# Epsilon folded into the variance aggregate, two-tensor row scalings and new instruction orders in a two-layer language-model tower

## The reference

```python
h = _L0_tok_ref(...)                      # word + position + type rows, layer norm (E), gamma, beta
h = h + _L0_attn_ref(_layernorm(h), ...)  # P: random-feature attention, 16 heads, 44 features
h = h + _L0_ffn_ref(_layernorm(h), ...)   # F: top-2 of 32 low-rank experts
h = h + _L1_attn_ref(_layernorm(h), ...)  # R: rotary causal softmax attention, 16 heads
h = h + _L1_ffn_ref(_layernorm(h), ...)   # M: ternary-weight MLP 256 -> 1024 -> 256
```

## Time and profile before

| | |
|---|---|
| median of 3 runs | 469.33 us (463.96 to 470.93) |
| the profiled execution: span from first to last instruction | 470.3 us (the page gives no other time of it) |
| TensorE busy | 401.4 us (85%) |
| VectorE busy | 366.7 us (78%) |
| GpSimd busy | 284.0 us (60%) |
| ScalarE busy | 257.9 us (55%) |

### The profile page before, as it was taken

The page is one execution under the profiler, slowest core; times in us unless marked ns, Lnnn a source line. Parts: engine busy times, 40 slices in busy tenths (PEclk is TensorE's granted clock), DMA queues, the critical chain, the costliest instruction groups (busy, mean ns, idle before and its releaser), DMA issues.

```text
span 470.3 us, 13968 instructions
## 1 busy us (share of the span) xinstructions
PE 401.4 (85%) x5026; PEld 273.4 (58%) x5026; DVE 366.7 (78%) x969; ACT 257.9 (55%) x573; POOL 284.0 (60%) x399
## 2 busy tenths in 40 slices
PE   8988768868898888799979797989898979797885
PEld 3444344535565667475747475656666656565664
DVE  4478899977999786999979698687878887766552
ACT  1246474547576555577738374647474736373541
POOL 7778888967577667677867655454555335252120
PEclk9998999979999899999989898898989998999999
DMA  4797542346464648455866484583767664611001
GB/s 135 183 291 189 144 102 26 70 100 106 102 118 92 116 91 140 106 119 96 138 113 107 96 121 88 94 152 68 95 104 127 116 91 74 101 36 24 13 13 35
DMA packets 145843, 48.55 MB, mean 103 GB/s; under 512 B 137264, under 2 KB 143216, under 8 KB 145776
## 3 DMA queue, kind: packets, MB, share of 16 engines
q1 hardware_dynamic: 144144, 43.21, 49.2%
q0 software_dynamic: 1632, 4.46, 3.4%
...
...
## 4 chain that ended last, share of the span: by engine, by line
PE 32%; issue 20%; DVE 15%; POOL 14%; DMA 9%; SPq 5%; ACT 4%; another core or an unknown queue 1%; POOLq 0%; DVEq 0%; ACTq 0%
PE PS L1415 11%; PE PS L2004 4%; PE PS L1925 2%; PE PS L2022 2%; DMA qkT<-qs 2%; DMA rTm<-split 2%; POOL split L695 2%; DMA rT<-split 1%; PE PS L1767 1%; PE PS L1626 1%; DVE xnR L1039 1%; DMA emb_type<-in_type,ids 1%; POOL qe L666 1%; SPq L534 1%
## 5 line engine op out<-in xcount | busy, mean ns | idle before, releaser
L1075 DVE TENSOR_REDUCE split<-PS 128x16 f16<-128x2048 f32 x16 | 36.8, 2297 | 10.3 <-PE PS L1494 7.6
L692 POOL TENSOR_TENSOR stage_f<-stage_f 128x512 f32<-128x512 f32 x16 | 21.0, 1310 | 27.7 <-DVE stage_f L1056 10.9
L1155 ACT ACTIVATE xTR<-PS 128x256 f16<-128x256 f32 x16 | 6.1, 382 | 49.6 <-PE PS L1805 49.6
L2004 PE MATMUL PS<-xTM,w1q 128*128 128x128 f16 x512 | 31.4, 219 | 0.0
L2004 PEld LDWEIGHTS PS<-xTM,w1q 128*128 128x128 f16 x512 | 28.6, 98 | 3.6 <-issue 3.6
L685 POOL TENSOR_TENSOR rstdR<-rstdR,consts 128x1 f32<-128x1 f32 x16 | 8.8, 553 | 32.9 <-DVE rstdR L1035 32.9
L666 POOL TENSOR_TENSOR qe<-qef,qe 128x704 f16<-128x704 f32 x16 | 25.3, 1580 | 5.4 <-ACT qe L1264 2.3
L1767 PE MATMUL PS<-faT_hi,hgT 128*128 128x256 f16 x128 | 25.8, 289 | 2.4 <-DMA hgT<-hgs 2.4
L1415 PE MATMUL PS<-rwqk_hi,xTR 128*128 128x512 f16 x64 | 27.2, 470 | 0.3
L1438 PE MATMUL PS<-warm 128*128 128x512 f16 x98 | 24.3, 415 | 1.4 <-DVE warm L1125 1.4
L1415 PE MATMUL PS<-wqkT_hi,xTP 128*128 128x512 f16 x64 | 23.9, 416 | 1.0 <-DMA xTP<-xsP 0.6
...
## 6 DMA issues: line engine op xcount, KB each, us to landing
...
rT<-split SPq DMA_TRANSPOSE x26, 3.6
```

What stands on the lines that cost most here:

```text
L692: g.tensor_tensor(rot[:, :, :].rearrange("p h d -> p (h d)"), rc[:, :], rs[:, :], ALU.add).then_inc(rot_ok, 1)
L1075: v.tensor_reduce(slots(SLOT - DH)[:, 0:H, DH - 1].rearrange("p (c j) -> p j c", j=4), PS[:, BANK["s1"]:BANK["s1"] + 4, :].rearrange("p j ...
L1155: return a.activation(dst, src, ACT.Copy)
L2004: last = pe.matmul(PS[:, BANK["m1"] + f // 4, f % 4 * P:(f % 4 + 1) * P], w1q[:, n % KC, f * P:(f + 1) * P], xT["M"][:, n, :], start=False ...
```

## The change

bn_aggr is given a third triple that never changes: count 0, mean 0 and a sum of squared deviations of 256 times epsilon. The variance that comes out already holds epsilon, and the additions go. `xnF` and `xnR` are written by a scalar_tensor_tensor: h minus the mean (a 128x1 pointer) times rstd, read as a second tensor that repeats its 128x1. All five orders are new, and `SPARE_WARM` loses its entry for `fQ` of tile 3.

```diff
-        stats = {x: sb(f"stats{x}", [P, 6]) for x in LNS}
+        triples = sb("triples", [P, len(LNS), 9])
+        stats = {x: triples[:, n, :] for n, x in enumerate(LNS)}
-        rstd = {x: sb(f"rstd{x}", [P, 2]) for x in LNS}
+        rstd = {x: sb(f"rstd{x}", [P, 1]) for x in LNS}
...
                 elif op == "Rrs":
-                    wait(g, ag_ok["R"], 3 * t + 3)
+                    wait(g, ag_ok["R"], 2 * t + 2)
                     wait(g, xn_ok["R"], t)
-                    g.tensor_tensor(rstd["R"][:, 1:2], rstd["R"][:, 0:1], consts[:, :], ALU.pow).then_inc(rs_ok["R"], 1)
+                    g.tensor_tensor(rstd["R"][:, :], mv["R"][:, 1:2], consts[:, :], ALU.pow).then_inc(rs_ok["R"], 1)
...
                 elif op == "Rst":
                     wait(v, hF_ok, t + 1)
-                    v.bn_stats(stats["R"][:, :], h_of(t)).then_inc(ag_ok["R"], 1)
+                    wait(v, ag_ok["R"], 2 * t)
+                    v.bn_stats(stats["R"][:, 0:6], h_of(t)).then_inc(ag_ok["R"], 1)
                 elif op == "Rag":
-                    wait(v, ag_ok["R"], 3 * t + 1)
+                    wait(v, ag_ok["R"], 2 * t + 1)
                     wait(v, xn_ok["R"], t)
-                    v.bn_aggr(mv["R"][:, :], stats["R"][:, :]).then_inc(ag_ok["R"], 1)
-                    wait(v, ag_ok["R"], 3 * t + 2)
-                    v.tensor_scalar(rstd["R"][:, 0:1], mv["R"][:, 1:2], RES_EPS, None, ALU.add).then_inc(ag_ok["R"], 1)
+                    v.bn_aggr(mv["R"][:, :], stats["R"]).then_inc(ag_ok["R"], 1)
                 elif op == "Rxn":
...
-                    v.tensor_scalar(xn["R"][:, :], h_of(t), mv["R"][:, 0:1], rstd["R"][:, 1:2], ALU.subtract, ALU.mult).then_inc(xn_ok["R"], 1)
+                    v.scalar_tensor_tensor(out=xn["R"][:, :], in0=h_of(t), scalar=mv["R"][:, 0:1], in1=bc(rstd["R"][:, :], [P, D]),
+                                           op0=ALU.subtract, op1=ALU.mult).then_inc(xn_ok["R"], 1)
...
+            v.memset(triples[:, :, 6:8], 0.0).then_inc(rows_set, 1)
+            v.memset(triples[:, 0:1, 8:9], D * EMB_EPS).then_inc(rows_set, 1)
+            v.memset(triples[:, 1:, 8:9], D * RES_EPS).then_inc(rows_set, 1)
...
 "SP":
-        lR qT PT lW1 qT qp lW2 PT qp qT PT qp qT hgT rT3 PT qp qT rT1 rT2 hgT onT rT3 qp PT qT rT2 rT1 hgT onT PT rT3 qp qT rT2 rT1 hgT onT rT3 qp PT
+        lW1 lW2 qT PT lR qT qp PT qp qT PT qp qT hgT rT3 PT qp qT rT2 rT1 hgT onT rT3 PT qp rT2 rT1 qT hgT onT rT3 PT qp qT rT1 rT2 hgT onT rT3
 "DVE":
-        Est Eag Est Eag zp1 Pst Pag zi zp4 zp3 PV Pst zp2 Pag zo1 qlo Est Eag diag zo2 zf1 qmx Est qb Eag qd Pst qlo kmx Pag kmr kb kd diag zo3 zf2
+        Est zi Eag Est Eag zm zp2 Pst zp3 zp1 Pag Pst Est Eag zo1 Pag PV qlo zp4 Est Eag zt zo2 Pst diag qmx Pag qb qd kmx Est kmr qlo kb kd
```

More of the change, by code:

```diff
@@ L67 @@
[L67 to L74, removed]
+        g g e2 g Ers e2 esc Ers eh e2 esc eh Prs Ers g Prs esc e2 eh Plo Ers g g e2 esc Prs qel Ers eh g e2 us Plo qel Frs esc Ers eh Prs dist
@@ new lines @@
+        g gsl hgl Plo uq1 uq2 Rrs esc Frs qel e2 Prs dist rot gsl rl Ers eh hgl uq4 uq3 esc Plo Rrs Frs Prs eh e2 qel dist rot rl gsl hgl Ers
+        onl Prs g qel Rrs Plo e2 Frs esc g rot eh rl dist Ers Mrs e2 gsl hgl esc onl Ers eh Prs Plo Rrs esc eh Frs g qel e2 rot dist rl g gsl
+        hgl onl g Plo Ers bb e2 Rrs Mrs Frs esc eh qel Prs rot dist rl g gsl hgl Ers rol onl Prs Plo bb Mrs e2 Rrs esc Frs Ers qel rot dist rl
+        Mrs rol gsl hgl onl Plo g Prs Rrs eh esc Frs Mlo e2 qel dist rot rl gsl Mrs hgl rol Ers bb onl g Rrs Mlo eh Plo Frs Prs esc qel rot
@@ new lines @@
+        dist eh Mrs rl bb gsl bb hgl onl Prs rol Plo e2 Prs Rrs Frs qel Mlo Ers bb dist rot esc rl gsl Plo hgl Mrs rol onl e2 qel Rrs Frs Ers
+        eh Mlo dist rot rl hgl Mrs gsl esc Plo rol onl bb Prs Rrs Frs eh qel Mlo Plo rot dist Mrs rl hgl rol gsl onl qel Rrs Frs Mlo rot dist
+        rl Prs bb Mrs hgl gsl onl rol Plo Mlo Rrs bb qel Frs rot dist rl Mrs bb gsl hgl rol Rrs Mlo Frs qel Mrs rot dist rl gsl hgl bb rol Mlo
+        Rrs Frs Mrs dist rot bb rl gsl hgl bb Mlo Rrs rot rl Mrs bb Mrs Mrs bb bb
@@ L111 @@
[L111 to L113 removed]
+        yp3 Exn yp2 Exn yp1 Pxn Pe Exn qhi Pxn Phi va sq ym1 yf2 Exn qhi qe2 qe1 yf1 sq ke kp yo Exn cth ym2 yf3 va qe1 Pxn Phi oe qe2 yr1 ke
@@ new lines @@
+        Fhi xsq kp qhi near tpf Pxn sq sec cth gsh va hgh yr2 Phi Exn hgTa oe qe1 qhi qe2 Rhi xsq Fhi ke kp near ym3 yr3 tpf sec cth Pxn gsh
+        rh1 sq rh2 rh3 hgh va rT2a Phi rT1a oe vr Exn qe2 qe1 ex2 Rhi xsq Fhi ex1 ke near kp qhi sec oh tpf rh1 rh3 sq gsh cth rh2 vr hgh va
+        onh Pxn Exn Phi qe1 re qe2 Rhi ex1 ex2 ke kp Fhi xsq rh1 rh2 rh3 qhi near oh cth tpf sec Exn va sq gsh hgh Pxn vr onh Phi Exn Mxn re
+        qe1 ex1 ex2 Rhi Me Pxn xsq qe2 Fhi ke oh kp qhi near rh1 mh1 rh2 sec tpf cth rh3 sq gsh mh2 hgh va Phi onh re qe1 Exn qe2 vr Rhi Mxn
@@ L157 @@
     "Ftr": {0: 2, 1: 5},
-    "fQ": {3: 3},
     "s1": {1: 7, 2: 3},
@@ L971, in step @@
                     wait(v, xsq_ok, t)
-                    v.tensor_scalar(xn["F"][:, :], h_of(t), mv["F"][:, 0:1], rstd["F"][:, 1:2], ALU.subtract, ALU.mult).then_inc(xn_ok["F"], 1)
+                    v.scalar_tensor_tensor(out=xn["F"][:, :], in0=h_of(t), scalar=mv["F"][:, 0:1], in1=bc(rstd["F"][:, :], [P, D]),
+                                           op0=ALU.subtract, op1=ALU.mult).then_inc(xn_ok["F"], 1)
                 elif op == "FT":
```

161 lines of the change are left out of this document (78 added, 83 removed).

## The result

The changed kernel takes **481.87 us** (median of 4 runs, 480.99 to 484.90); the kernel before, timed beside it, 468.26 (4 runs, 463.96 to 470.93). The ratio is 1.033 [1.028, 1.039]. The forecast was 463.0 with a range of 455 to 472, and the case that came nearest, *the start decides*, had a chance of 0.07 and a price of 473. The ratios leave disturbed executions out and the means given further on take all of them, so the two can differ, most for one kernel (old_orders, 1.014 against 1.001).

What follows compares the result with a forecast made beforehand. TensorE and VectorE were taken to bound the middle in turn. 470.3 - 2.5 - 1.4 - 3.5 + 1.0 = 463.9 for the profiled execution, which is 1.0 above the median: forecast 463.0 us, range 455 to 472.

Steps and rivals of the forecast that it cites:

- the start decides: Rival, start: first qkT transpose queues behind W1 and W2, all later stages up to 6 us later; 473 us, chance 0.07.
- the start term: Start of the kernel: first aggregate behind set-up zi, first q/k product at about 28 instead of 27.0; +1.0 us.
- first features after 40 us: Sign of being wrong, start: the first feature matmul, at 35.52 before, starts after about 40 us.
- The orders: GpSimd's neighbour of the R power: no qe subtraction behind it any more, so xnR runs free; 1.4 us won.
- TensorE's clock I leave as it is: TensorE between 40 and 420 us: granted clock taken as unchanged, with 3 us either way left to the range.
- The two gains of the middle, 2.5 and 3.5 us: Additions gone: 2.5 us from TensorE's waits for xnR and xnF, 3.5 from its other waits on VectorE.
- Nothing arrives: Rival: DMA waits and TensorE's own 90% late on take over wherever VectorE is sooner; 467 to 469 us, chance 0.18.
- Two signs of being wrong: TensorE's idle time still at 69 us, and its waits now named after DMAs.
- the aggregate's price: VectorE's aggregate reading nine values instead of six: taken to cost nothing more, at most 6.9 us in all.
- The scaling waits for GpSimd: Two-tensor xnR and xnF: 0.41 us free, end 0.28 after a GpSimd operation; about +1 us of VectorE time.
- the 15 of the forecast: VectorE's busy time over the whole run: to fall from 366.7 to about 352 us.

Runs made afterwards that it cites:

- old_orders: The changed kernel with the order table of the kernel before, and its three warming matmuls ahead of fQ of tile 3: mean 469.2 us, ratio 1.014.
- exn_first: The changed kernel with only ScalarE's first Exn put back ahead of its wait for the q/k bias row: mean 482.7 us, ratio 1.037.
- the filled kernels: More warming matmuls put in TensorE's waits: 105 in the changed kernel, mean 473.9 us; 34 in the kernel before, mean 465.4 us.
- old_to_r0: The changed kernel with every engine in the old order up to the R normalisation of tile 0, then the new order: mean 474.7 us, ratio 1.016.
- new_to_r0: The changed kernel with every engine in the new order up to the R normalisation of tile 0, then the old order: mean 481.3 us, ratio 1.030.

## Why the prediction was wrong

**Three terms failed, by about as much each.** The forecast has +1.0 us for the start, -1.4 for the orders behind it, and -2.5 - 3.5 for the additions. In the means the start costs 7.7 (482.4 - 474.7), the orders behind it 5.5 (474.7 - 469.2), and the edits 0.5 (469.2 - 468.7): 6.7, 6.9 and 6.5 us worse than forecast, 20 us together. How the last two share their 6.0 us (474.7 - 468.7) leans on the mean of old_orders; their sum and the start's 7.7 do not.

**The step that failed first is the start term**, "+1.0 us; bounds: -1 ... and +6". I followed one chain, from the first aggregate to the first q/k product, put it at about 28 us instead of 27.0, and let the slack behind the warm-up matmuls hide the rest. The product came at 31.62. I had missed ScalarE's new order, where the first Exn stands behind the wait for the bias row: with Exn ahead of it (exn_first) the product comes at 28.66. I had also missed GpSimd's, where the gather of tile 3 is issued at some 30 us behind W1 and W2 (it was at 25 before), so that VectorE's queue stands behind esum. But neither repair brought any time back, so what failed is the method too: the start is not one chain that ends in the first product. Measured by prefix, the start costs 7.7 us in front of the new rest and 12.1 in front of the old, above the bound of 6. Its own sign of failure, "first features after 40 us", was met nearly (39.84). The rival *the start decides* named the right place, and mis-sized it: it had 6.1 us for it, and in the profiled run it was 11.6 at tile 0.

**"The orders", 1.4 us, was priced at one neighbour and stands for more.** The neighbour itself was right: xnR's mean fell from 754 to 613 ns, with the old form even to 518, and TensorE's waits for it from 9.4 to 4.4 us (5.5 forecast). But this is one of some fifty waits that a new order changes. The rest of the new order costs 5.5 us behind the old start. Its lag builds up between tiles 2 and 7, and TensorE waits there 6.8 us for rT and 3.6 for hgT, where the kernel before waits 0.6 for rT, 1.6 for rTm and nothing for hgT. These waits go with the new rest and not with the start: over the whole run they are 9.1 and 7.8 us in old_to_r0, 4.4 and 1.9 in new_to_r0. That they are the cause is not shown; no run takes them away alone.

**"TensorE's clock I leave as it is"**, with "3 us either way", was another error. By the filled kernels it counts some 5 us here, in one direction: a long wait costs its own length and then half speed behind it, as at 25.3 to 35.7 us above.

**The two gains of the middle, 2.5 and 3.5 us, did not arrive.** eps_only has nothing but the additions' removal, and is at 467.1 against 468.7. Which engine takes over where VectorE is sooner was not traced. *Nothing arrives* (0.18) is what the epsilon edit does by itself. Two signs of being wrong bear on it and were met: TensorE's idle time did not fall (77.6 us), and its two largest waits are now named after DMAs.

**Right:** the aggregate's price was taken as nothing and is 14 ns (191 against 177), 1 us in 80, far under the bound of 6.9. The scaling waits for GpSimd and ends 0.28 us behind it. Its free duration was off: 0.46, not the 0.41 of the PSUM-to-SBUF row. The Trainium skill (VectorE: DVE Perf Modes, the perf-mode tier table) has the one-tensor form at two elements per cycle and a two-tensor form at one, by which I had estimated 0.13 us more; the least durations (397 and 462 ns) show half of that. VectorE's sum fell 5.6 us and not the 15 of the forecast. The additions' 12.0 us went; the aggregates took 1.2 back, and the two scalings together 0.6: xnR fell by 2.3 us, but xnF rose from 11.3 to 14.2, since four of its tiles now run into a qe subtraction nearly from its start (1.60 to 1.74 us each; I had counted three). Most of the rest is set-up that takes longer in its new place: one copy into fb 3.10 us against 0.21.
